# The order of the first-layer products in the feed-forward stages of a three-stage layer: four low-weight products first, then the high-weight pairs

## The reference

```python
x = x + 0.5 * ffn(layernorm(x), Wr, br, W1, b1, W2, b2)
x = x + attn(layernorm(x), query_proj, key_proj, value_proj, output_proj)
x = x + 0.5 * ffn(layernorm(x), Wr, br, W1, b1, W2, b2)

# in ffn: the two best of 8 experts weigh in, but every expert is computed for every token
probs = softmax(flat @ Wr + br); vals, idx = top_k(probs, 2)
w = vals / (sum(vals) + EPS)
for e in range(8):
    we = sum(w * (idx == e))
    hmid = gelu(flat @ W1[e] + b1[e])        # 128 -> 512
    y = hmid @ W2[e] + b2[e]                 # 512 -> 128
    out_acc += we[:, None] * y
```

## Time and profile before

| | |
|---|---|
| median of three runs | 784.38 us (782.45 to 784.77) |
| the profiled execution | 784.93 us |
| its span | 783.1 us |
| TensorE (PE) busy | 772.8 us, 99% of the span |
| VectorE (DVE) busy | 675.6 us, 86% |
| ScalarE (ACT) busy | 615.7 us, 79% |
| GpSimd (POOL) busy | 200.1 us, 26% |
| granted TensorE clock, mean | 0.997 of full speed |

### The profile page before, as it was taken

How to read it: one execution, slowest core, us unless ns; L and a number is a source line. 1 busy time by engine, 2 the same in 40 slices (tenths; PEclk the granted TensorE clock), 3 DMA queues, 4 the chain that set the end, 5 groups by cost and what they waited for, 6 DMA issues and landing times.

```text
span 783.1 us, 11801 instructions
## 1 busy us (share of the span) xinstructions
PE 772.8 (99%) x3642; PEld 464.5 (59%) x3642; DVE 675.6 (86%) x1348; ACT 615.7 (79%) x1018; POOL 200.1 (26%) x261
## 2 busy tenths in 40 slices
PE   9999999999999999999999999999999999999998
PEld 5778888888772333333333332333498788888886
DVE  7897878789768999999999999999547888878886
ACT  4886767676667999999999999999715767776763
POOL 2117523333301111111111112111112046333331
PEclk9999999999999999999999999999999999999999
DMA  7031312110473111111311111120000024101111
GB/s 206 28 112 54 108 54 107 55 54 1 161 280 98 54 55 54 55 54 54 108 55 55 54 55 54 54 82 1 2 1 1 28 112 157 59 40 68 55 54 54
DMA packets 25413, 54.65 MB, mean 70 GB/s; under 512 B 5264, under 2 KB 10768, under 8 KB 23312
## 3 DMA queue, kind: packets, MB, share of 16 engines
q1 hardware_dynamic: 25360, 54.00, 20.4%
HBM read 44.42 MB, written 9.57 MB: 69 GB/s over the span
## 4 chain that ended last, share of the span: by engine, by line
PE 92%; DVE 5%; ACT 2%; issue 1%; POOL 0%; DVEq 0%
PE ps L979 30%; PE ps L967 11%; PE ps L410 7%; PE ps L411 7%; PE ps L399 7%; PE ps L412 7%; PE ps L401 7%; PE ps L400 7%; PE ps L986 4%; PE ps L168 1%; DVE hlo L688 1%; ACT ef L1056 1%; DVE hhi L684 1%; PE ps L379 1%; PE ps L954 1%
## 5 line engine op out<-in xcount | busy, mean ns | idle before, releaser
L1120 DVE TENSOR_SCALAR_CACHE_REDUCE ef<-ps 128x1024 f32<-128x1024 f32 x256 | 307.3, 1214 | 8.2 <-PE ps L967 1.5
L1056 ACT ACTIVATE ef<-ef,nmax 128x1024 f32<-128x1024 f32 x256 | 293.9, 1148 | 10.5 <-DVE ef L1120 3.8
L979 PE MATMUL ps<-ef,vs 128*64 128x512 f32 x1024 | 249.4, 608 | 0.2
L495 ACT ACTIVATE ps<-ps,b_sb 128x512 f32<-128x512 f32 x256 | 169.2, 664 | 88.2 <-PE ps L401 86.2
L688 DVE TENSOR_TENSOR hlo<-ps,hhi 128x512 fp32r<-128x512 f32 x256 | 165.6, 686 | 4.1
L979 PEld LDWEIGHTS ps<-ef,vs 128*64 128x64 f32 x1024 | 62.8, 136 | 121.0 <-issue 108.4
L684 DVE CAST hhi<-ps 128x512 fp32r<-128x512 f32 x128 | 87.7, 685 | 46.8 <-ACT ps L495 46.7
L1164 POOL TENSOR_TENSOR vs<-V,rsum 128x128 f32<-128x128 f32 x128 | 51.1, 400 | 295.9 <-DVE rsum L1126 295.9
L544 POOL TENSOR_TENSOR acc<-acc,ysc 128x512 f32<-128x512 f32 x55 | 70.7, 1288 | 150.8 <-DVE ysc L711 150.1
L399 PE MATMUL ps<-xhi,w1lo 128*128 128x512 f32 x256 | 101.9, 398 | 0.8 <-DVE hlo L688 0.8
L410 PE MATMUL ps<-hhi,w2lo 128*128 128x512 f32 x256 | 100.9, 394 | 0.8 <-DVE gT L762 0.8
(11 more groups left out here) (102 smaller groups left out, 672.7 us busy)
## 6 DMA issues: line engine op xcount, KB each, us to landing
gb<-gates SPq DMA_DIRECT2D x16, 1024.0 KB, 4.6
qs<-qk_parts SPq DMA_DIRECT2D x32, 256.0 KB, 3.3
ks<-qk_parts SPq DMA_DIRECT2D x32, 256.0 KB, 3.9
w1raw<-in_w SPq DMA_DIRECT2D x16, 256.0 KB, 4.5
w2raw<-in_w SPq DMA_DIRECT2D x16, 256.0 KB, 4.8
qk_parts<-sthi SPq DMA_DIRECT2D x16, 256.0 KB, 2.2
qk_parts<-stlo SPq DMA_DIRECT2D x16, 256.0 KB, 2.7
xt<-in_x SPq DMA_DIRECT2D x4, 256.0 KB, 3.8
```

The source lines that it names most:

```text
L495: nc.scalar.activation(bank(mc), bank(mc), ACT.Gelu, bias=b1_sb[:, u, mc:mc + 1]).then_inc(F.gelu, 1)
L979: last = nc.tensor.matmul(bank(6 + half)[x * VD:(x + 1) * VD, :], vs[:, t % VRING, x * VD:(x + 1) * VD], ef[:, (2 * t + x) % ERING, half * ...
L1056: nc.scalar.activation(ef[:, c, :], ef[:, c, :], ACT.Exp, scale=-1.0, bias=nmax[:, c:c + 1], accum_out=esum[:, c:c + 1]).then_inc(s_exp, 1)
L1120: nc.vector.tensor_scalar(ef[:, c, :], bank(slot_bank(u), 2), -1.0, None, ALU.mult, ALU.min, accum_out=nmax[:, c:c + 1]).then_inc(s_max, 1)
```

## The change

In `hidden` the one loop over the four chunks becomes two. The first issues the low-weight product of every chunk, each behind its wait on `F.lo`; the second issues the two high-weight products of chunk 0, then of chunk 1, 2 and 3. Each product keeps its operands and its bank. The line numbers after it move by 4 (L399 becomes L402, L400 and L401 become L404 and L405, L410 becomes L414, L457 becomes L461).

```diff
+                cols = slice(tt * 512, (tt + 1) * 512)
+
+                def w(mc):
+                    return slice(mc * P, (mc + 1) * P)
+
                 for mc in range(MC):
                     if not (isinstance(i, int) and i == 0 and s == 0):
                         pe.wait_ge(F.lo, i * 32 + (4 * s + mc - 3 + L0))
-                    w = slice(mc * P, (mc + 1) * P)
-                    cols = slice(tt * 512, (tt + 1) * 512)
-                    nc.tensor.matmul(bank(mc), w1lo[:, u, w], xhi[:, cols], start=True, stop=False)
-                    nc.tensor.matmul(bank(mc), w1hi[:, u, w], xlo[:, cols], start=False, stop=False)
-                    nc.tensor.matmul(bank(mc), w1hi[:, u, w], xhi[:, cols], start=False, stop=True).then_inc(F.h, 1)
+                    nc.tensor.matmul(bank(mc), w1lo[:, u, w(mc)], xhi[:, cols], start=True, stop=False)
+                for mc in range(MC):
+                    nc.tensor.matmul(bank(mc), w1hi[:, u, w(mc)], xlo[:, cols], start=False, stop=False)
+                    nc.tensor.matmul(bank(mc), w1hi[:, u, w(mc)], xhi[:, cols], start=False, stop=True).then_inc(F.h, 1)
```

## The result

The changed kernel took 806.7 us as the median of four runs (806.43 to 809.01), against 784.43 us before on the same chip. The ratio is 1.0289, with a 95% interval of 1.0273 to 1.0305: 2.9% slower. The forecast was 806.5, in a range of 796 to 814. The profiled execution took 806.43 us with a span of 804.6, at a mean granted clock of 0.994 (before: 784.93, 783.1 and 0.997).

A forecast was written before the change was run, and what follows sets the result against it. TensorE's issue rate was taken to bound the feed-forward stages, so any wait adds time. Terms 8.3 + 8.8 + 3.5 + 0.5 + 1.0 = 22.1 us gave 807.0 on the profiled execution, 806.5 as median; range 796 to 814.

The forecast's parts named there:

- The steady stretch: Units 6 to 30 of both stages: TensorE stalls 0.15 or 0.22 us between units, period 5.69 instead of 5.54; 8.3 us.
- 0.70 later: Hidden: bank 0 completes behind the 6th matmul instead of the 3rd, moving gelu and VectorE's chain 0.70 us later.
- 1.40 earlier: Hidden: bank 3 is asked for at the 4th matmul instead of the 10th, 1.40 us earlier.
- the handover: At a wait for a bank, the waiting matmul acts as if started 0.16 us after the freeing `hlo` ends.
- the slack of 0.01: Steady stretch: of bank 3's 2.11 us of slack, 0.01 remains after spending 0.70 and 1.40.
- Rival A: Only the first pairs lose; the steady stretch keeps its period of 5.54; 798 us, chance 0.17.
- The first pair of experts: Longer waits for bank 3: units 4 to 6 of both stages 8.8 us, units 1 and 2 together 3.5 us.
- The end of the first stage: Transposes of the normalised data start later because VectorE's queue behind unit 30's chain moves by 0.70; 0.5 us.
- The clock: Long stalls in unit 4 of each stage make the granted clock fall, 0.5 us a stage; 1.0 us, bounds 0 to 4.8.
- B: More is lost: steady handover or chain longer by 0.15, or clock falls behind all long stalls; 810 to 816 us, chance 0.13.
- C: Not slower: TensorE goes past a waiting low product to bank 0's high products; 781 to 786 us, chance 0.03.
- D: The clock swings in the steady stretch, as the skill's rule says; some 27 us more, 834 us, chance 0.02.

The follow-up runs named there:

- e2: Kernel before, hidden reordered so bank 0 completes behind the 6th matmul as in the change, bank 3 still asked for at the 10th; 792.71 us.
- e4: The change with one matmul moved: bank 0 complete behind the 7th matmul instead of the 6th, bank 3 still asked for at the 4th; 821.84 us.
- e1: Kernel before, hidden reordered so bank 3 is asked for at the 4th matmul as in the change, bank 0 still complete behind the 3rd; 794.52 us.
- e3: The change with one matmul moved: bank 3 asked for at the 5th matmul instead of the 4th, bank 0 still complete behind the 6th; 798.05 us.
- e5: Changed order only in the first pair of experts of both stages (units 0 to 8), order of before in the rest; 800.52 us.
- e8: The change plus the early gelu table load of e7, and the router's steps one instead of two at a time between unit 3's chunks; 804.39 us.
- e6: Order of before in the first pair of experts of both stages, changed order in the other three pairs; 792.23 us.
- e7: The change plus a one-column gelu behind the router's exponential on ScalarE, to load the gelu table early; 805.2 us.

## Why the prediction was right

- **The steady stretch** (8.3 us). Right in each of its parts: 0.70 later (e2, e4), 1.40 earlier (e1, e3), the handover of 0.16, the slack of 0.01 between them. The period is 5.69, and units 7 to 31 added 4.2 us a stage, as forecast. e3 and e4 show that this is the sum and not either part: one slot to the one side and the period is 5.54, one to the other and it is 5.92. Rival A is out by the rows. That a slack of 0.01, a difference of rows read to 0.01, came out to the hundredth is in part luck.
- **The first pair of experts** (8.8 and 3.5 us). Right in the second stage to 0.1 us for each unit. In the first, units 4 to 6 added what was forecast, but the clock moved it: unit 4 to 5 added 3.7 instead of 2.1, unit 5 to 6 0.4 instead of 1.9. That the slow matmuls behind unit 4 would be taken out of unit 5's wait had been said. Unit 2 added 1.2 as forecast. Unit 1, read in e5 at full clock, added 1.4 (1.5 forecast), but 0.4 of it at its first low product, which waits for bank 0; the forecast had the wait at bank 3 alone. That unit 5's wait hangs on the table load is borne out by e8, in which both edits together save what was expected at full clock; the load by itself was not measured at full clock.
- **The end of the first stage** (0.5 us). The stretch from unit 31 to the second stage added 0.5, in the change and in e6, and nothing in e5. In the change 0.2 of it stands where the forecast had it, at the transposes of the normalised data (L206); another 0.2 stands at transposes of `acc` (L176) that wait for GpSimd, which the forecast did not name.
- **The clock** (1.0 us). The size came out in the profiled execution and the place did not, which is luck. The forecast had 0.5 behind unit 4 of each stage. Behind unit 4 the clock fell in one stage of two, and the fall cost nothing; the 1.0 was lost in unit 1 of the first stage. The profiled execution added 21.5 us in all, 22.4 less the 0.9 by which its unit 0 began earlier.
- **The clock in the other runs.** One minus the mean clock, times the span, is the time that the slow stretches would cost if no wait hid any of it: 0.8 to 3.1 us for before, 3.2 to 7.3 for the four runs of the change, 2.4 to 8.7 for those of e1. If this is taken off each run of e1, 797.09 at 0.989 and 790.67 at 0.997 come to 788.3 both. It is an upper bound: the change took 806.77 at 0.996, but 806.64 and 809.01 at 0.991, so its times do not follow the mean clock. How much of the 22.3 us between the medians is clock is open. The price of a long wait is the wait and, in some executions, a fall of the clock, which costs where no wait follows. I had priced the falls by one row of before and not their number, and the expectations of e1 to e5, e7 and e8, which had 1.0 us for it or nothing, came out 1 to 4 us too low.
- **Slots.** No change of bank cost anything: the eight high products, which change the bank every second time, keep a slot of 0.233.
- **What would show it.** The sentence that TensorE's waits for `hlo` would total 15 us or more was wrong as a reading of the view: the table has 6.7, because waits below the drain of the matmul ahead are counted as busy.
- **Rivals.** B did not come in full: the steady stall was 0.15, and of the four long stalls two had a fall behind them, of which one cost time. C needed TensorE to go on past a waiting product; the rows of unit 4 show it issuing in order. D did not occur: the stretches from 61 to 199 and from 655 to 785 us read a clock of 1.00, with a wait of 0.15 to 0.24 in each unit of the steady stretch. The rule of the Trainium skill (TensorE: Matmul & The Clock Gate, "A second HAM failure mode: psum-queue depth-cycling") was that short idle pieces between groups make the clock swing; at this size they did not.

## What to carry to other kernels

When an engine that is 99% busy hands work to others and takes a buffer back, count two things for a new order: how much later the first product of a group is complete, and how much earlier the last buffer is asked for. Their sum against the slack decides, in a threshold: below it a reordering costs nothing in that stretch, above it each slot is paid in every unit (e3 and e4, one slot to either side). The places with less slack than the steady stretch (here the router and the table load) pay first and most, and the steady row alone does not show them.

## What the runs showed of the hardware

- A wait of a matmul that is shorter than the drain of the one ahead does not appear as idle time. It lengthens the row: four low products in one row of 1.24 us with a wait of 0.15 among them, 1.09 without.
- From the end of the instruction that frees a bank to the second matmul behind the wait it took 0.38 to 0.40 us at full clock, against 0.23 without a wait, in the long waits and the short ones alike.
- The granted clock fell to the level of 1.2 GHz (slots of 0.43 us) within 1 us after TensorE had been busy for 2.23 of 4 us, and had returned some 3.4 us later (slow from 43.4 to 46.8). In the second stage of the same execution the same waits of unit 4, with the same busy time, left it at 2.4 GHz. What decides between the two is open.
- A fall of the clock cost 1.0 us where the engine had no wait behind it (unit 1) and nothing where it had one (unit 4).
- A table load stood behind the wait for the operand of the gelu that needed it (43.38, behind bank 0). Issued early, by a gelu of one column, it stood at 40.20, before that operand came.
